# Attention weights folded ahead of the layers, and unscaled queries in a recurrence, in a two-block network on one core

## The chip, the cores and the metric

The kernel runs on one core of a Trainium2 chip. Its five engines (TensorE or PE, VectorE or DVE, ScalarE or ACT, GpSimd or POOL, SyncE or SP) each work through a list of their own, in order, and meet through semaphores. The metric is the device time of one execution in microseconds. The kernel before took 655.72 us (median of 3 runs, 652.77 to 656.79).

## The reference

The input x is 2 sequences of 1024 tokens of width 128, all in float32. Two blocks follow each other, each of the form x + attention(norm x) + experts(norm x).

```
# block 0
xn = layernorm(x)
q, k, v = xn Wq', xn Wk', xn Wv'
w[t,s] = exp(log(sigmoid(xn Wd' + bd) + 1e-8)[s] * max(s-t-1, 0)) * (s > t)
attn = ((q k' / sqrt(128)) * w) v Wo' * out_scale
ffn = xn, through 4 layers of: idx, p = top1(softmax(h @ router[l])) of 16 experts
                               h = p * silu(h @ W1[idx]) @ W2[idx]      (512 wide)
x = x + attn + ffn
# block 1
xn = layernorm(x);  ctrl = xn @ W_ctrl + b_ctrl      (9 parts)
q, k, v = silu(causal depthwise conv, 4 taps)        (16 heads of 8)
q = q / sqrt(sum(q*q) + 1e-12);  k likewise
per token: vec = u * rotate(vec @ W_block, angle) + (1-u) * silu(cand)
           S   = alpha * S + beta * k (v - S'k)';  read = S' q
attn = [rms(read) * w_m, rms(vec) * w_v] @ W_out + b_out, times sigmoid(gate)
ffn = p * (xn @ expert[top1]' + b)   of 8 experts
x = x + attn + ffn
```

Two identities matter to the change. Products of weights can be taken ahead: x Wq' (x Wk')' = (x Wq'Wk) x', and (x Wv') Wo' = x (Wo Wv)'. And rms(read) of a scaled query is read / sqrt(mean(read*read) + 1e-6 * (sum(q*q) + 1e-12)) of the unscaled one.

## The kernel before

**Front of block 0.** The 2048 tokens are 16 tiles of 128, in 4 groups of 4. SyncE loads x in four parts, then W2 in four parts (experts 0 to 1, 2 to 5, 6 to 10, 11 to 15), clears a scratch of 2 MB in HBM (`sorted_x<-slotbuf`), and loads W1 (4 MB). ScalarE issues nine small loads ahead of all else (L1682 to L1687: Wq, Wk, Wv, Wo, the first router, Wd, the later routers, bd, out_scale), 0.45 us each to issue and 0.68 for bd, which is spread over partitions. VectorE takes statistics (L975, L978) and scales rows (L988), group after group; GpSimd meanwhile makes constants (L703 the last long one).
TensorE's list starts when all nine loads have landed: transposes of the four attention weights (L2339), of tokens (L2126), the first layer's logits (L2135), ranks, and then a turn for each of 16 experts: transposes of W2 (L2222, copied by ScalarE at L1761) and W2 times the later routers (L2233, copied in turns by VectorE and ScalarE), so that each layer's output brings the next layer's logits with it. From expert 6 on a turn holds one of twelve attention products (L2247 queries and keys, L2250 values; VectorE copies them, L1119). VectorE also chooses and places each token by expert, and GpSimd scatters the rows into expert order (L737).

**Layers.** Each of 4 layers walks 31 tiles of 128 rows of sorted tokens: load, transpose (L2308), 8 products with W1 (L2317), SiLU, 8 with W2 (L2332), scatter (L748, L753). Between tiles stand pieces of the attention: scores (L2260), decay weights, retrieve (L2270), and the output product with Wo (L2283), 15 times, which VectorE adds to x (`attention_added`, L1244).

**Front of block 1.** GpSimd adds the expert rows to x, group by group; VectorE takes the mean (L1371, L1372), ScalarE the squares (L1879) and roots (L1698), VectorE scales (L1381), TensorE transposes and projects into the conv inputs (L2436, biased and copied by ScalarE at L1862). VectorE runs six convolutions (q, k and v for each of 2 sequences, each of three instructions of L1400 and L1403), with the angle range reduction after the second (L1422 to L1426, five instructions), then one rotation plane (`turn_plane`, L1414), the decay inputs (L1432) and the other plane. The recurrence is held with 32 chunks of 64 tokens on partitions: TensorE brings keys, queries and values into that form in four pieces each (`chunks`, L2451: 32 products of 128 partitions with a half of the identity); ScalarE squares (L1873) and copies them (L1874), GpSimd sums the squares (L820 to L822), ScalarE takes roots (L1935), VectorE reciprocals (L1442). GpSimd scales all queries by theirs (L847) before its first step.

**Recurrence.** 32 steps. In each VectorE computes prediction, difference and new state (L1510 to L1551), ScalarE the decayed state (L1948, eight pieces), GpSimd state times query (L864), TensorE sums it (L2561). Planes of the vector scan, routing (L1472 to L1493), experts (L2509, L2525) and gate stand between the steps at numbers written out by hand. GpSimd runs the vector scan (L784 to L790) from step 8 on. Behind the steps come a scan over chunks (L2670), corrections, mean squares, and the output projection.

## Time and profile before

| | us | share of span |
|---|---|---|
| median of 3 runs | 655.72 | |
| the profiled execution | 655.12 | |
| its span | 653.0 | |
| TensorE products | 566.2 | 87% |
| TensorE weight loads | 479.6 | 73% |
| VectorE | 475.1 | 73% |
| ScalarE | 427.5 | 65% |
| GpSimd | 383.4 | 59% |

The trace is of one execution; 2.1 us of its time lie outside the span. DMA moved 39.85 MB. Busy shares are means over stages with different limits; the slices show them: columns of 16.3 us each, tenths of the slice.

```profile
## 2 busy tenths in 40 slices
PE   0889999999999899989999589876965977798896
...
DVE  6655458865688457874312699799999999997946
ACT  1563567746675467645686688978877887786443
POOL 5354045710475025734555323786999999998984
PEclk9989999999999999979999698968979887989999
```

TensorE is full from the second slice to the twenty-second, VectorE from the twenty-fifth, GpSimd from the twenty-ninth. The chain that ended last gives TensorE 51%, GpSimd 21%, VectorE 18%.

### The profile page before, as it was taken

The page shows a single profiled execution, that of the slowest core. Times are in us where ns is not written, and L with a number is a line of the kernel's source. Part 1 is how long each engine was busy: PE and PEld are TensorE (multiplying, and loading weights), DVE is VectorE, ACT ScalarE, POOL GpSimd, SP SyncE. Part 2 cuts the span into 40 slices and gives each one's busy share as a digit, 9 for nine tenths or more (in the row PEclk, how much of TensorE's full clock was granted, in tenths as well). Part 3 has the DMA queues.
Part 4 walks back from the last instruction along what each step waited for, and adds up shares of the span by engine and source line. Part 5 has one row for each costly group of instructions (what it writes and reads, how often), then busy time and mean ns, then how long its engine had stood idle before and what let it go on. Part 6 is the DMA issues. An engine that isn't in the chain of part 4 may idle for free.

```text
span 653.0 us, 14371 instructions
## 1 busy us (share of the span) xinstructions
PE 566.2 (87%) x4639; PEld 479.6 (73%) x4639; DVE 475.1 (73%) x1380; ACT 427.5 (65%) x1032; POOL 383.4 (59%) x434
## 2 busy tenths in 40 slices
PE   0889999999999899989999589876965977798896
PEld 0767999769995899959997357744744755586785
DVE  6655458865688457874312699799999999997946
ACT  1563567746675467645686688978877887786443
POOL 5354045710475025734555323786999999998984
PEclk9989999999999999979999698968979887989999
DMA  8944553136321653125322000000000000000002
GB/s 291 346 149 47 161 120 66 55 58 166 74 65 46 92 147 65 54 55 74 71 53 77 23 1 2 1 2 1 1 0 2 1 1 1 1 2 1 3 2 66
DMA packets 104122, 39.85 MB, mean 61 GB/s; under 512 B 85906, under 2 KB 96178, under 8 KB 103922
## 3 DMA queue, kind: packets, MB, share of 16 engines
q1 hardware_dynamic: 98018, 29.34, 19.9%
q0 software_dynamic: 4480, 9.30, 4.2%
q8 instruction: 40, 0.66, 0.4%
q10 hardware_dynamic: 1552, 0.30, 0.2%
q14 instruction: 32, 0.26, 0.1%
HBM read 20.32 MB, written 18.59 MB: 60 GB/s over the span
## 4 chain that ended last, share of the span: by engine, by line
PE 51%; POOL 21%; DVE 18%; ACT 4%; issue 3%; DMA 2%; ACTq 1%; POOLq 0%; DVEq 0%; SPq 0%
PE PS L2332 17%; PE PS L2317 16%; POOL W1s L864 9%; DVE W2s L1403 4%; POOL wT L784 4%; PE PS L2270 2%; PE PS L2233 2%; POOL two_planes L786 2%; POOL slotbuf L788 2%; DMA oscale<-in_L_attn_out_scale_dram 2%; PE PS L2260 1%; ACT W1s L1948 1%; POOL hbuf L790 1%; POOL two_planes L789 1%; PE PS L2670 1%
## 5 line engine op out<-in xcount | busy, mean ns | idle before, releaser
L748 POOL DMA_INDIRECT sorted_x<-xrow,pos x93 | 90.9, 977 | 134.6 <-DVE pos L1216 107.8
L2332 PE MATMUL PS<-W2s,hbuf 128*128 x992 | 139.3, 284 | 0.0
L2317 PE MATMUL PS<-hbuf,swt 128*128 128x128 f32 x992 | 131.7, 276 | 1.0 <-DVE hbuf L1281 0.9
L2332 PEld LDWEIGHTS PS<-W2s,hbuf 128*128 128x128 f32 x992 | 126.7, 191 | 0.5
L2317 PEld LDWEIGHTS PS<-hbuf,swt 128*128 128x128 f32 x992 | 120.9, 192 | 1.6 <-issue 0.9
L1733 ACT ACTIVATE hbuf<-PS 128x512 f32<-128x512 f32 x124 | 73.2, 590 | 45.6 <-PE PS L2317 44.4
L1741 ACT ACTIVATE xrow<-PS,tags 128x144 f32<-128x144 f32 (+1 forms) x124 | 46.9, 378 | 41.8 <-PE PS L2332 39.6
L1948 ACT ACTIVATE W1s<-W1s,ab 128x128 f32<-128x128 f32 x168 | 51.3, 393 | 15.4 <-DVE W1s L1551 15.3
L2509 PE MATMUL PS<-ewT,xT 128*128 128x512 f32 x64 | 38.6, 734 | 21.0 <-ACT W2s L1999 21.0
L864 POOL TENSOR_TENSOR W1s<-W1s,kT 128x1024 f32<-128x1024 f32 x22 | 52.4, 2388 | 7.0 <-DVE W1s L1551 5.8
L753 POOL DMA_INDIRECT results<-xrow,pos x31 | 31.2, 1007 | 37.1 <-ACT xrow L1741 25.1
L1275 DVE COPY swt<-W1s 128x512 f32 x64 | 27.2, 427 | 35.2 <-PE PS L2317 33.2
L1284 DVE STREAM_TRANSPOSE hbuf<-hbuf 128x128 f32<-128x128 f32 x116 | 33.4, 301 | 23.0 <-DMA hbuf<-sorted_x 22.2
L2525 PEld LDWEIGHTS PS<-W2s,ident 128*128 128x128 f32 x256 | 34.9, 212 | 12.7 <-issue 12.4
L2561 PE MATMUL PS<-ident,W1s 128*128 128x128 f32 x256 | 34.8, 280 | 6.2 <-POOL W1s L864 6.2
L1815 ACT ACTIVATE swt<-W1s 128x512 f32 x60 | 37.9, 631 | 3.0 <-issue 1.0
L1999 ACT ACTIVATE W2s<-PS,selbuf 128x128 f32<-128x128 f32 x128 | 35.3, 370 | 5.0 <-issue 4.6
L2509 PEld LDWEIGHTS PS<-ewT,xT 128*128 128x128 f32 x64 | 12.9, 223 | 32.6 <-ACT W2s L1999 22.7
L2525 PE MATMUL PS<-W2s,ident 128*128 128x128 f32 x256 | 34.7, 294 | 2.0 <-DVE xres L1465 2.0
L2561 PEld LDWEIGHTS PS<-ident,W1s 128*128 128x128 f32 x256 | 29.2, 143 | 8.2 <-POOL W1s L864 7.5
L1948 ACT ACTIVATE W1s<-xrow,ab 128x128 f32<-128x128 f32 x88 | 26.9, 394 | 8.8 <-DVE xrow L1551 8.8
L1235 DVE SCALAR_TENSOR_TENSOR wdec<-PS,wdec 128x512 f32<-128x512 f32 (+3 forms) x24 | 13.4, 557 | 22.0 <-PE PS L2260 21.5
(419 smaller groups left out, 1324.4 us busy)
## 6 DMA issues: line engine op xcount, KB each, us to landing
hbuf<-sorted_x SPq DMA_DIRECT2D x224, 32.0 KB
sorted_x<-slotbuf SPq DMA_DIRECT2D x9, 520.0 KB, 2.9
W1s<-in_L_ffn_W_dram SPq DMA_DIRECT2D x1, 4096.0 KB, 20.6
sorted_x<-slotbuf SPq DMA_DIRECT2D x1, 2015.0 KB, 11.2
sorted_x<-xrow,pos POOLq DMA_INDIRECT x109, 2.4
sorted_x<-slotbuf SPq DMA_DIRECT2D x3, 455.0 KB, 2.8
xres<-in_L_attn_x_dram SPq DMA_DIRECT2D x4, 256.0 KB, 4.1
xrow<-results SPq DMA_DIRECT2D x4, 256.0 KB, 4.1
```

The costliest lines, as they stand in the source:

```text
L748: pool.indirect_dma_start(xs_dram[l + 1][:, :], bass.IndirectOffsetOnAxis(ap=pos[:, t:t + 1], axis=0), xrow[:, t % NR, 0:XW], None).then_i ...
L864: pool.tensor_tensor(qX[t % QR], X[(t + 1) % NX], Qc[:, t, :, :].unsqueeze(1).to_broadcast([P, 2 * HD, HP, HD]), ALU.mult).then_inc(r_read ...
L1733: act.activation(hTs[:, (c - 1) % 2, :], PS[:, 2 + (c - 1) % 2, :], ACT.Silu).then_inc(h_act, 1)
L1741: act.activation(xrow[:, t % NR, 0:w], PS[:, 4 + c % 2, 0:w], ACT.Copy, scale=tags[:, t, 1:2]).then_inc(y_ev, 1)
L1815: act.activation(w1st[:, c % WB, :], W1s[:, bass.ds(w, FF)], ACT.Copy).then_inc(w1_act, 1)
L1948: o = act.activation(aX[:, :, h, :], X[t % NX][:, :, h, :], ACT.Copy, scale=ab[:, t, h:h + 1])
L1999: o = act.activation(scaled[:, t % 2, e, :], PS[:, 4 + e // 4, e % 4 * D:(e % 4 + 1) * D], ACT.Copy, scale=sel[:, t, e:e + 1])
L2317: m = pe.matmul(PS[:, 2 + n, f * P:(f + 1) * P], w1st[:, (c - 1) % WB, f * P:(f + 1) * P], xring[:, (c - 1) % R, :], start=True, stop=True)
L2332: m = pe.matmul(PS[:, 4 + n, 0:w], hTs[:, n, f * P:(f + 1) * P], W2s[:, f * YW:f * YW + (E - 1) * NF + w][:, bass.ds(w2, w)], start=(f == ...
L2509: m = pe.matmul(PS[:, 4 + n, :], xT[:, t * P:(t + 1) * P], ewT[:, n * 512:(n + 1) * 512], start=True, stop=True)
L2525: pe.matmul(o, ident[:, :], scaled[:, t % 2, e, :], start=(e == 0), stop=False)
L2561: m = pe.matmul(o, qXw[t % QR][:, i, :], ident[:, :], is_transpose=True, start=(i == 0), stop=(i == HD - 1))
```

## The change

In the front, four small loads stay ahead (first router, Wd, bd, out_scale); the four attention weights and the later routers are issued by ScalarE after its table load, between its first roots, with a semaphore of their own. TensorE starts with tokens; then it waits for these five and makes Wq'Wk and a transpose of Wo (`folded_weights`), later Wo Wv (`folded_values`). The twelve attention products become eight: four give queries times the folded product, four give values times the folded one; ScalarE copies the first four, VectorE the rest. Scores take the tokens `xT` for the keys. The output product with Wo becomes a transpose. A long constant instruction of GpSimd waits for two scaled groups.

In block 1, norm groups 0 and 1 take their statistics on VectorE, with no squares on ScalarE, and group 0 ahead of an attention sum. Two of five range instructions go to GpSimd. The four key chunks stand together ahead of the third conv input, and a chunk is made of one 64x64 transpose and one 64x64 product a step. The decay inputs move ahead of the sixth convolution, the rotation planes into steps 2 and 3, the planes of the vector scan from steps 3 to 6 to 4 to 7. Queries stay unscaled: their lengths, reciprocal and scaling go; GpSimd squares them at step 1, TensorE sums them for step 4, and the sums, times 1e-6, are added into the mean squares.

```diff
+    QUERY_EPS_AT = 4
+    TURN_PLANE_AT = {2: 1, 3: 3}
...
+            pool.wait_ge(layer_x, 2)
...
-            pool.wait_ge(sincos, 2)
-            pool.tensor_tensor(cosp, cosp, cosp, ALU.mult).then_inc(cos_ready, 1)
-            squared_lengths(0)
+            pool.wait_ge(ang_red, 1)
+            step(pool.tensor_scalar(cosp, kp, -TWO_PI_LO, None, ALU.mult))
+            step(pool.tensor_tensor(angp, angp, cosp, ALU.add))
+            pool.tensor_scalar(angp, angp, PI_DOWN, -PI_DOWN, ALU.min, ALU.max).then_inc(ang_red, 1)
+            squared_lengths()
...
-            squared_lengths(1)
-            plane_summed(0)
-            pool.wait_ge(unit_ready, 2)
-            q_all = Qc.rearrange("p t h i -> p (t h) i")
-            step(pool.tensor_tensor(q_all, q_all, nstd[:, 1, :].unsqueeze(2).to_broadcast([P, C * HP, HD]), ALU.mult))
...
+                if t % (C // NG) == 0:
+                    pool.wait_ge(pa_ev, JOB_EV[f"q{t // (C // NG)}"])
...
+            dve.wait_ge(w_tr, 1)
+            dve.tensor_copy(wT[:, 0::3, :], PS[:, 5, :].rearrange("p (n d) -> p n d", n=4)[:, 0::3, :]).then_inc(w_ready, 1)
             first_place(0)
...
+            row_means(0)
             attention_added(4)
-            row_means(0)
             row_means(1)
+            row_scaled(0)
             attention_added(5)
             row_means(2)
-            row_scaled(0)
+            row_scaled(1)
             row_means(3)
-            row_scaled(1)
             row_scaled(2)
             row_scaled(3)
...
+            conv(0)
+            conv(1)
+            dve.wait_ge(pa_ev, 2)
+            step(dve.tensor_scalar(kp, angp, 1.0 / TWO_PI, ROUND, ALU.mult, ALU.add))
+            step(dve.tensor_scalar(kp, kp, ROUND, None, ALU.subtract))
+            dve.scalar_tensor_tensor(out=angp, in0=kp, scalar=-TWO_PI_HI, in1=angp, op0=ALU.mult, op1=ALU.add).then_inc(ang_red, 1)
+            conv(2)
+            conv(3)
+            conv(4)
+            decay_inputs()
+            conv(5)
+            key_lengths()
...
-            for n, w in enumerate(("Wq", "Wk", "Wv", "Wo")):
-                act.dma_start(wraw[:, n, :], ins[f"L0_attn_{w}"][:, :]).then_inc(ld_small, 16)
             act.dma_start(rw0[:, 0:E], routers[0, :, :]).then_inc(ld_small, 16)
...
+                if g < BY_STATS:
+                    act.wait_ge(centred, NG + g + 1)
+                    act.activation(stat[:, 2, tt], ex[:, tt, 7], ACT.Sqrt, bias=eps_ln[:, 0:1]).then_inc(ln_std, 1)
...
             preload(ACT.Sqrt)
+            own_weights(0)
+            own_weights(1)
             first_root(0)
+            own_weights(2)
+            own_weights(3)
             first_root(1)
+            act.dma_start(rw[:, 0:L - 1, :], routers[1:L, :, :].rearrange("l d e -> d l e")).then_inc(ld_own, 16)
             tokens_T(0, 0)
...
+            silu(1)
+            for g in range(NG):
+                chunked(0, Kc, g)
             conv_input(2, 0)
             conv_input(2, 1)
             silu(2)
-            chunked(0, Kc, 2)
             conv_input(2, 2)
             conv_input(2, 3)
             silu(3)
-            chunked(0, Kc, 3)
-            act.wait_ge(cos_ready, 1)
-            for n in (1, 3):
-                w = slice(n, n + 1)
-                act.activation(cos_part[n], cosp, ACT.Identity, bias=wblk[:, w], scale=n2wblk[:, w]).then_inc(cos_ready, 1)
-            silu(4)
-            silu(5)
+            act.wait_ge(ang_red, 2)
+            act.activation(cosp, angp, ACT.Sin, scale=0.5).then_inc(sincos, 1)
+            act.activation(sinp, angp, ACT.Sin).then_inc(sincos, 1)
+            preload(ACT.Sqrt)
+            lengths()
+            preload(ACT.Silu, 1)
...
+                if t == QUERY_EPS_AT:
+                    act.wait_ge(pd_mm, 6)
+                    act.activation(query_eps, PS[:, 1, 0:NT * H], ACT.Identity, scale=1e-6, bias=eps_q[:, 0:1]).then_inc(len_ready, 1)
...
-                    m = pe.matmul(PS[:, 7, t * P:(t + 1) * P], retT[:, (u % 2 * HB + t) * P:(u % 2 * HB + t + 1) * P],
-                                  wT[:, 3, :], start=True, stop=True)
+                    m = pe.transpose(PS[:, 7, t * P:(t + 1) * P], retT[:, (u % 2 * HB + t) * P:(u % 2 * HB + t + 1) * P], ident[:, :])
...
+            def folded_weights():
+                pe.wait_ge(ld_own, 16 * 5)
+                pe.matmul(PS[:, 5, 0:D], wraw[:, 0, :], wraw[:, 1, :], start=True, stop=True)
+                pe.transpose(PS[:, 5, 3 * D:4 * D], wraw[:, 3, :], ident[:, :]).then_inc(w_tr, 1)
+            def folded_values():
+                pe.wait_ge(w_ready, 1)
+                pe.wait_ge(xt_ready, 2)
+                pe.matmul(PS[:, ATTN_BANKS[0], 0:D], wraw[:, 2, :], wT[:, 3, :], start=True, stop=True).then_inc(w_tr, 1)
             pe.wait_ge(consts, 1)
-            pe.wait_ge(ld_small, 16 * 9)
-            for n in range(4):
-                m = pe.transpose(PS[:, 5, n * P:(n + 1) * P], wraw[:, n, :], ident[:, :])
-            m.then_inc(w_tr, 1)
             tokens_T(0, 0)
+            pe.wait_ge(ld_small, 16 * 4)
+            logits(0)
+            tokens_T(0, 1)
             second_T(0)
-            tokens_T(0, 1)
-            logits(0)
-            second_T(1)
+            folded_weights()
             pe.wait_ge(consts, 3)
-            second_routers(0)
             first_ranks(0)
             logits(1)
-            second_T(2)
+            second_T(1)
+            second_routers(0)
+            tokens_T(0, 2)
+            folded_values()
             second_routers(1)
-            tokens_T(0, 2)
             first_ranks(1)
-            second_T(3)
-            second_routers(2)
+            attention_in(0)
             tokens_T(0, 3)
-            second_T(4)
-            second_routers(3)
             logits(2)
-            second_T(5)
-            second_routers(4)
-            first_ranks(2)
-            for e in range(QKV_FROM, E):
+            for e in range(2, 6):
                 second_T(e)
-                second_routers(e - 1)
-                qkv(e - QKV_FROM)
-                if e == QKV_FROM + 2:
+                attention_in(e - 1)
+                second_routers(e)
+                if e == 2:
+                    first_ranks(2)
+            for e in range(6, E):
+                second_T(e)
+                if e > 6:
+                    second_routers(e - 1)
+                if e - 1 < 2 * NG:
+                    attention_in(e - 1)
+                if e == 8:
                     tile_row(0)
             second_routers(E - 1)
-            qkv(E - QKV_FROM)
-            qkv(E - QKV_FROM + 1)
-            pe.wait_ge(qkv_ready, 3 * NG)
+            pe.wait_ge(attn_ready, 2 * NG)
...
-                        for q in range(HS):
-                            m = pe.matmul(o[part_rows(q), t * DP:(t + 1) * DP], v, ident[:, part_rows(q)], start=True, stop=True)
+                        a, z = part_rows(0), part_rows(1)
+                        pe.transpose(o[a, t * DP:(t + 1) * DP], v[a], ident[a, a])
+                        m = pe.matmul(o[z, t * DP:(t + 1) * DP], v[z], ident[z, z], start=True, stop=True)
...
+            alpha_beta(range(8, 14))
+            chunks(0, range(NG))
             conv_input(2, 0)
             conv_input(2, 1)
-            chunks(0, (2,))
+            alpha_beta(range(14, 20))
             conv_input(2, 2)
             conv_input(2, 3)
-            chunks(0, (3,))
-            alpha_beta(range(10, C))
-            chunks(1, (0,))
+            alpha_beta(range(20, C))
+            chunks(1, range(NG))
...
+                if t == QUERY_EPS_AT - 1:
+                    pe.wait_ge(sq_ready, NG + 1)
+                    pe.wait_ge(sh1, 1)
+                    for n in range(NT):
+                        m = pe.matmul(PS[:, 1, n * H:(n + 1) * H], query_squares[:, n * P:(n + 1) * P], headsel[:, :], start=True, stop=True)
+                    m.then_inc(pd_mm, 1)
...
+                pe.matmul(PS[:, half, 0:G * H], ident[:, :], query_eps[:, half * G * H:(half + 1) * G * H], start=True, stop=False)
                 for t in range(G):
                     tt = half * G + t
-                    r = P // H
-                    m = pe.matmul(PS[:, half, t * H:(t + r) * H].rearrange("p (r h) -> p r h", r=r),
-                                  osq[:, tt * P:(tt + 1) * P], headmean[:, :].unsqueeze(1).to_broadcast([P, r, H]),
-                                  start=True, stop=True)
+                    m = pe.matmul(PS[:, half, t * H:(t + 1) * H], osq[:, tt * P:(tt + 1) * P], headmean[:, :], start=False, stop=(t == G - 1))
```

## Rows read from the trace of the kernel before

**Rows 1.** Chain of waits, first 68 us: start us, us, what.
```profile
4.87 9.99 DMA oscale<-in_L_attn_out_scale_dram
...
53.12 0.89 PE PS L2247 x2
54.01 0.44 PE PS L2222 x4
54.44 0.87 PE PS L2233 x8
```

**Rows 2.** Stage windows: stretch, length, busy (instructions) of five engines, clock, DMA, GB/s.
```profile
35.80:39.00 3.20, 3.20 (x24) 3.06 (x21) 2.54 (x12) 0.88 (x3) 0.00 (x0) 0.50 0.60 224
39.00:64.00 25.00, 23.98 (x166) 18.92 (x164) 12.92 (x35) 14.41 (x29) 14.32 (x43) 1.00 0.34 50
```

**Rows 3.** Timeline of the front: start us, us, engine, line, operation.
```profile
5.36 1.28 ACT L1724 ACT_TABLE_LOAD   x1 [5.36 <-issue]
...
7.37 2.44 DVE L988 TENSOR_SCALAR xrow<-xres,ex,stat 128x128 f32<-128x128 f32 x4
...
8.69 2.79 POOL L703 TENSOR_SCALAR dist<-hbuf 128x1024 f32<-128x1024 int32 x1
...
11.10 1.11 DVE L988 TENSOR_SCALAR xrow<-xres,ex,stat 128x128 f32<-128x128 f32 x4
...
64.11 0.44 PE L2308 MATMUL PS<-ident,hbuf 128*128 128x128 f32 x2 [0.78 <-DVE vtok L1119]
```

**Rows 4.** DMA: ScalarE's queue in 8:10 and 10:12 us; issues, us to landing.
```profile
q10 hardware_dynamic: 649, 0.02, 20.2%
...
q10 hardware_dynamic: 7, 0.00, 0.2%
...
sorted_x<-slotbuf SPq DMA_DIRECT2D x1, 2015.0 KB, 11.2
...
W1s<-in_L_ffn_W_dram SPq DMA_DIRECT2D x1, 4096.0 KB, 20.6
...
wraw<-in_L_attn_Wq_dram ACTq DMA_DIRECT2D x1, 64.0 KB, 2.3
```

**Rows 5.** Groups by line, ScalarE, 15 to 64.5 us: busy, mean ns, idle before.
```profile
L1761 ACT ACTIVATE retT<-PS 128x512 f32<-128x512 f32 x16 | 9.5, 593 | 15.1 <-PE PS L2222 15.0
```

**Rows 6.** Groups by line, TensorE, 138 to 352 us.
```profile
L2283 PE MATMUL PS<-wT,retT 128*128 128x128 f32 x30 | 4.0, 275 | 0.0
```

**Rows 7.** Chain of waits, 360 to 405 us.
```profile
362.28 3.19 ACT xT L1879 x16
...
375.47 1.29 DVE W2s L1403
...
404.87 1.42 DVE slotbuf L1414
```

**Rows 8.** Groups by line, VectorE, 374 to 415 us.
```profile
L1432 DVE TENSOR_TENSOR abraw<-PS,abbias 64x256 f32<-64x256 f32 x4 | 1.7, 422 | 0.1
...
L1425 DVE SCALAR_TENSOR_TENSOR retT<-dist,retT 128x1024 f32<-128x1024 f32 x1 | 1.2, 1226 | 0.0
L1426 DVE TENSOR_SCALAR retT<-retT 128x1024 f32<-128x1024 f32 x1 | 0.7, 697 | 0.0
```

**Rows 9.** Timeline of the second block.
```profile
385.58 4.27 PE L2451 MATMUL PS<-ident,W2s 128*64 128x64 f32 x64
...
415.30 0.69 DVE L1539 TENSOR_TENSOR W1s<-W1s,PS 128x512 f32<-128x512 f32 x1
...
424.48 1.75 DVE L1442 RECIPROCAL wraw<-wraw 128x256 f32<-128x256 f32 x1
...
448.08 2.38 POOL L864 TENSOR_TENSOR W1s<-W1s,kT 128x1024 f32<-128x1024 f32 x1 [5.76 <-DVE W1s L1551]
...
474.61 2.40 POOL L864 TENSOR_TENSOR W1s<-W1s,kT 128x1024 f32<-128x1024 f32 x1
...
607.75 0.29 PE L2670 MATMUL PS<-xT,W1s 64*64 64x64 f32 x4
```

More of the change, by code:

```diff
@@ L147, in build @@
     HALF = S // 512
[L148 removed]
+    assert ROUTE_AT < KB and B * NC * HS == P and B * (D // 2) == P and OFF[-1] == NCTRL
     assert at == C - 1 and len(EXPERTS_AT) == len(SUMS_AT) == NT and halves == 2 * NT
@@ L729, in second_block_masks @@
                 step(pool.memset(eps_col[:, :], 1e-6))
+                step(pool.memset(eps_q[:, :], 1e-18))
                 pool.memset(eps_kq[:, :], 1e-12).then_inc(consts1, 1)
@@ L866, in _ @@
                 if t < VEC_AT:
-                    if t == 2:
+                    if t == 0:
+                        pool.wait_ge(sincos, 2)
+                        pool.tensor_tensor(cosp, cosp, cosp, ALU.mult).then_inc(cos_ready, 1)
+                    elif t == 1:
+                        pool.wait_ge(post_ready, 2 * B)
+                        for b in range(B):
+                            half = slice(b * S, (b + 1) * S)
+                            o = pool.tensor_tensor(query_squares[:, half], post[1][:, half], post[1][:, half], ALU.mult)
+                        o.then_inc(sq_ready, 1)
+                    elif t == 3:
+                        plane_summed(0)
                         plane_summed(1)
@@ L1310, in _ @@
             route_tiles(0, NFG)
-            later_router(4)
-            for e in range(QKV_FROM, E):
-                qkv(e - QKV_FROM)
-                if e % 2 == 0:
-                    later_router(e)
-                if e == QKV_FROM + 2:
+            for e in range(4, E, 2):
+                for n in (e - 1, e):
+                    if BY_ACT <= n < 2 * NG:
+                        attention_in(n)
+                later_router(e)
+                if e == 8:
                     tile_table(0)
@@ L1415, in turn_plane @@
                                               op0=ALU.mult, op1=ALU.add))
-            dve.wait_ge(consts1, 3)
-            for k in range(3 * B):
-                conv(k)
-                if k == 1:
-                    dve.wait_ge(pa_ev, 2)
-                    step(dve.tensor_scalar(kp, angp, 1.0 / TWO_PI, ROUND, ALU.mult, ALU.add))
-                    step(dve.tensor_scalar(kp, kp, ROUND, None, ALU.subtract))
-                    step(dve.scalar_tensor_tensor(out=angp, in0=kp, scalar=-TWO_PI_HI, in1=angp, op0=ALU.mult, op1=ALU.add))
-                    step(dve.scalar_tensor_tensor(out=angp, in0=kp, scalar=-TWO_PI_LO, in1=angp, op0=ALU.mult, op1=ALU.add))
-                    dve.tensor_scalar(angp, angp, PI_DOWN, -PI_DOWN, ALU.min, ALU.max).then_inc(ang_red, 1)
@@ L1436, in _, with decay_inputs @@
-            o.then_inc(pd_ev, 1)
-            dve.wait_ge(conv_done, 3 * B)
-            def unit(n):
-                dve.wait_ge(len_ready, 2 * n + 2)
-                dve.reciprocal(nstd[:, n, :], nstd[:, n, :]).then_inc(unit_ready, 1)
-                dve.wait_ge(unit_ready, n + 1)
+            def decay_inputs():
+                dve.wait_ge(pd_mm, 4)
+                for q in range(HS):
+                    for k in range(2):
+                        half = part_rows(k)
+                        o = dve.tensor_tensor(abraw[part_rows(q), k * C // 2:(k + 1) * C // 2, :].rearrange("p t (n h) -> p t n h", n=2),
+                                              PS[half, 6, :].rearrange("p (t n q h) -> p q t n h", n=2, q=HS, h=HP)[:, q, :, :, :],
+                                              abbias[half, q, :].rearrange("p (n h) -> p n h", n=2).unsqueeze(1)
+                                              .to_broadcast([DP, C // 2, 2, HP]), ALU.add)
+                o.then_inc(pd_ev, 1)
@@ L1445, in next_keys, with key_lengths @@
+            def key_lengths():
+                dve.wait_ge(len_ready, 2)
+                dve.reciprocal(nstd, nstd).then_inc(unit_ready, 1)
+                dve.wait_ge(unit_ready, 1)
             def next_keys(t):
@@ L1954, in _, with rotation @@
             decayed(0)
-            for g in range(1, NG):
-                chunked(1, Qc, g)
+            def rotation(n):
+                if n == 0:
+                    act.wait_ge(sincos, 2)
+                    for i in range(2):
+                        act.activation(mpl[:, 0, i, :], sinp, ACT.Copy, scale=nwblk[:, 2 * i + 1:2 * i + 2]).then_inc(sincos, 1)
+                    return
+                for m in ((1, 3), (0, 2))[n - 1]:
+                    w = slice(m, m + 1)
+                    act.wait_ge(cos_ready, 1 if n == 1 else 3 + m // 2)
+                    act.activation(cos_part[m], cosp, ACT.Identity, bias=wblk[:, w], scale=n2wblk[:, w]).then_inc(cos_ready, 1)
             def plane_banks():
@@ L2014, in _ @@
                     reads_evac(t // G - 1)
+                if t in (0, 2, 3):
+                    rotation((t + 1) // 2)
+                if t in (1, 4):
+                    plane(zpl[:, t // 4, :], ACT.Silu, pbias[:, 2 + t // 4:3 + t // 4])
                 if t == 1:
-                    lengths(1)
-                if t in (2, 3):
-                    value(t - 1)
-                if t in (1, 2):
-                    plane(zpl[:, t - 1, :], ACT.Silu, pbias[:, 1 + t:2 + t])
+                    value(1)
+                elif t == 4:
+                    value(2)
+                    value(3)
                 if t == ROUTE_AT + 1:
```

249 lines of the change are left out of this document (124 added, 125 removed).

## The prediction, made before the result was known

> **What bounds the kernel now.** I read the slices of the page first, then the chain of waits, then for three stretches the stage windows, the timelines and the groups by line. Four stretches follow each other. (a) The front, to 64.11 us, where the first transpose of the first layer's tiles starts [rows 3]. TensorE does nothing until 14.99: its first instruction waits for all nine small loads of ScalarE's queue, and the last of them, oscale, takes 9.99 us to land [rows 1]. From 39 to 64 TensorE is busy 23.98 of 25 us at full clock [rows 2]; what ends there is its own list, turn after turn of 0.89 + 0.44 + 0.87 us [rows 1]. (b) Four layers to 352 us, TensorE busy from end to end. (c) The second block's front to 415.30, where the first state is written [rows 9]: the chain runs over VectorE's convolutions and then over ScalarE. (d) The recurrence, in which VectorE leads for nine steps and GpSimd from 474.61 [rows 9] to about 595, and the scan behind it. A gain in (a), (b) or (c) comes out at the end; in (d) it counts only if GpSimd starts earlier.
>
> **Front: the start.** Only four small loads stand ahead of the table load now: 0.45 + 0.45 + 0.68 + 0.45 us of issue (the 0.68 is the load spread over partitions) from 0.8, so to 2.9 us. Table load 1.28 [rows 3] and its 0.20: 4.4. Two weight loads are issued (0.95), then the root (0.3): 5.65. VectorE's statistics of two groups end at 6.4. Scaling of the first group took 2.44 us beside GpSimd's 2.79 us instruction at 8.69 [rows 3]; that one now waits for two groups, and the four scalings cost the 1.11 of the later groups. With the reciprocal: tokens at 7.8. TensorE: transposes 0.85 at the cold rate, copy 0.6, logits 0.85, second tokens 0.85, first W2 expert 0.5 to 0.9: about 12 us. What was done at 19.5 before is done at 12.
>
> **Front: the new wait.** Then TensorE waits for five loads (four weights, later routers), the last issued at 7.0 to 7.45. Behind that wait, in TensorE's order, stand ranks, logits and every later transpose; in VectorE's order the weight copy stands ahead of the first placing. The trace shows no load of this queue issued so late. From below: 7.45 + the 2.3 us of a weight load [rows 4] = 9.7, and TensorE would not notice. From above: oscale shows what happens to a tail that meets the 2 MB clearing transfer: 649 packets of this queue move in 8 to 10 us, 7 in 10 to 12 [rows 4]; the clearing lands at 4.06 + 11.2 = 15.3, oscale at 14.86. Behind it W2's stream keeps the engines full, so up to 18. I take **16**, nearest to oscale's row.
>
> The Trainium skill (DMA: Bandwidth & Descriptors, Queues, rings and completion order) says that each engine alternates between its queues packet by packet, whole packets of several descriptors. By it the 24 rows per engine of the last load want only two or so turns after the clearing: near 16 to 17, the same sum; it speaks against the slow rival below, as oscale's landing does.
>
> **Front: TensorE's list from there.** Fold and transpose 0.3, ranks 1.25 in all, logits 0.87 + 1.74, 15 W2 transposes at 0.44 = 6.6, 16 router products at 0.87 = 13.9, eight attention products at 0.89 = 7.1 (twelve before: keys are gone, 3.6 us), tokens 0.9, folded values 0.25, tile row 0.3: 33.2, so 49.2. The waits between: tokens and logits for ScalarE's copies 0.9; ScalarE's three table loads and two decays fall in turns that lost their attention product, 2.0 + 0.6 per turn against TensorE's 1.31, and cost it 1.3; hot masks and first copies 1.1; the last router copy 0.7. That gives 53.2. After an idle stretch the clock was 0.50 in 35.8 to 39 [rows 2]; a like phase after the new wait, about 1 us: **54.2**. Laid out in the same manner with these prices, the order before gives 64.2 (trace 64.11). Placing ends at 34.5, its last eight scatters at 1.27 us each at 44.7, tiles load 3 to 5 us later: covered, and so is W1, which lands at 39.8 [rows 4]. ScalarE has 0.6 [rows 5] plus half a router copy of 0.5 per turn: also under 1.31. So −9.9, with bounds −13.3 (landing before 13) and −7 (18, and a longer cold phase).
>
> **Layers.** 30 records of the output product [rows 6] become 15 transpose records; either kind runs at 0.11 us per record (0.87 for 8 products, 0.44 for 4 transposes [rows 1]). TensorE is the path there: −1.6; bounds 0 and −1.7. Scores read xT for kT: the same shapes, nothing.
>
> **Second block, norms.** For groups 0 and 1 the path was sum, negation, eight squares of 0.39 + 0.19 (3.19 us [rows 7]); now 1.25 us of statistics on VectorE, and group 0 no longer stands behind the attention sum. The first convolution still waits for groups 2 and 3, which keep the old way: start at 375.3 [rows 7] less 1.5.
>
> **Second block, convolutions.** Six of three instructions of 1.29 us [rows 7] stay. Two range instructions, 1.23 + 0.70 [rows 8], go to GpSimd, idle then; the decay inputs, 4 x 0.42 [rows 8], move ahead of the sixth; two plane turns (1.42 [rows 7] and 1.3) move into steps 2 and 3. The four key chunks now all stand ahead of the third conv input on TensorE and ScalarE: if a chunk costs what it did (64 records in 4.27 us for two [rows 9]: 2.15), the fifth convolution starts about 4.5 us late. The new form has 24 records on a 64x64 corner. The nearest row by shape is the scan's, 4 records on such a corner in 0.29 us with the next corner's beside them, some 0.03 us per record [rows 9]: 0.7. Bounds 0.7 and 2.15; I take 0.9, since transposes and products alternate between two corners as there. ScalarE's 1.05 per chunk is then longer, and VectorE loses 0.3 us.
>
> The Trainium skill (TensorE: Matmul & The Clock Gate, Part 3, The mechanism) has weight loads run beside products only on other row groups. Its Part 4 says that transposes do not count as busy for the clock. Here 0.44 per four transposes at granted clock 1.00 stands beside products; alone they would be a rival, below.
>
> From the sixth convolution to the first state: silu, value chunk, copy, eight decays of 0.3, 7 us. Against 415.30 that is −4.5 (with the norms). **Steps 1 to 4**: from 417.8 to 448.03 before, 30.2; now four of 5.07, routing 1.0, keys 0.45, choice 3.95, two turns 2.8: 28.5, since the query reciprocal (1.75 [rows 9]), the 3.8 us query scaling and its waits are gone. Steps 4 to 7 give about 2 back: the planes come one step later and ScalarE (2.45 + 2.1 + a 1.28 table load, values) is late for VectorE. GpSimd had no gap from 448.08 to 474.61 [rows 9]; it takes up two squares (4.8), the second sum and the cosine square earlier, while it waited anyway. Laid out so, step 9 starts at −4.3; the same layout gives 472.3 for 474.61 before. I take **−4**; bounds −6 (GpSimd alone) and +3 (chunks at 2.15). Behind it nothing moves; the mean squares have 10 short records for 8 long ones: 0.
>
> **Sum.** 655.1 (the profiled execution; 0.6 under the median of 655.7) −9.9 −1.6 −4 = **639.6**. A measurement tells about 1%, 6.6 us, from no change.
>
> **Rivals.**
> - *The late weights* (slower). If the five loads had to wait for the W2 and W1 stream to end, at 39.8, TensorE's list would start there: 54.2 + 23.8 = 78.0, that is +13.9 −5.6 = +8.3: 663. It breaks even at a landing of 31.5. For: the queue's 7 packets in 2 us. Against: oscale landed while W2 still streamed, and scatters landed in 2.3 to 5.3 us beside it. 6%.
> - *Nothing from the second block*: chunks near 2.15, or ScalarE late: +3 there: 646.6. For: ScalarE has hardly a gap in 404 to 420. 24%.
> - *The slow clock*: with attention products gone, turns 9 to 15 are half transposes; at 0.50, as in 35.8 to 39 [rows 2], their 9.2 us double: 648.8. Against: 39 to 64 is 1.00 with the same transposes. This is what the skill's Part 4 would make of it. 10%.
> - *The weights in time* (landing before 13): 3.4 more: 636. 15%.
> - The forecast: 45%.
>
> Range 633 to 650: below, the early weights with the full −6; above, either of the two middle rivals. Faster by over 1%: 0.89; within: 0.05 (two middle rivals together); slower: 0.06.
>
> **What would show it.** The first transposes near 8, the fold product near 16, the first layer near 54; 15 transpose records for the output; chunks at 16 transposes or products and 0.7 to 0.9 us; first state write near 399 on the new clock (415.3 −11.5 −4.5), GpSimd's ninth step 15.5 us earlier. A fold product after 20, a clock of 0.5 between 40 and 54, or VectorE waiting long for conv inputs would make it wrong.

## The result: slower by 4.4%, and where it went

The changed kernel takes 683.88 us (median of 4 runs, 682.69 to 684.68) against 654.76 (now 4 runs); the ratio is 1.044, with a 95% interval of 1.040 to 1.048, written [1.040, 1.048] below. The forecast was 639.6. Its profiled execution has a span of 681.4 us against 653.0: 28.4 us more. The page's slices of the changed kernel, columns of 17 us:

```profile
PE 612.8 (90%) x4554; PEld 504.6 (74%) x4554; DVE 467.8 (69%) x1381; ACT 425.2 (62%) x1019; POOL 385.2 (57%) x436
...
PE   2899999999999999999969999999867777798896
...
DVE  7644568755885578742067533488999999997936
...
PEclk9999999999999999899988575666998779989997
```

TensorE has 85 fewer records and 47 us more of work. In the slices that follow the layers it is full, its granted clock is at 5 to 8 tenths, and VectorE drops to 2 and 0. The waits of VectorE that end after 390 us and the timeline of TensorE name the place. Columns of the waits: who waited for whom, us in total, times, longest.

```profile
DVE PS L1545 <- ACT vtok L1944: 18.7, 1, 18.7
DVE W2s L1432 <- ACT W2s L1916: 17.4, 1, 17.4
```

Two waits, 36 us: the fifth convolution waits for its input, which stands behind the four key chunks, and the first step waits behind the four query chunks. The timeline of TensorE inside a key chunk, at its start and at its end:

```profile
376.59 0.27 PE L2517 MATMUL PS<-ident,W2s 64*64 64x64 f32 x1 [0.38 <-ACT W2s L1922]
376.79 0.43 PE L2518 MATMUL PS<-ident,W2s 64*64 64x64 f32 x2
377.14 0.27 PE L2517 MATMUL PS<-ident,W2s 64*64 64x64 f32 x1
...
396.67 0.32 PE L2517 MATMUL PS<-ident,W2s 64*64 64x64 f32 x1
396.92 0.48 PE L2518 MATMUL PS<-ident,W2s 64*64 64x64 f32 x2
397.32 3.78 PE L2502 MATMUL PS<-xT,wc 128*128 128x512 f32 x4
```

L2517 is the transpose, L2518 the product. A plain float32 product shows as two records, a transpose as one. One step takes 0.55 us at first and 0.66 later; a chunk 5.25, where it took 2.15 and 0.9 was forecast. The conv inputs behind the chunks run at half rate (3.78 us for four records; 1.98 in the trace of before). The stage windows, to be read as [rows 2]:

```profile
375.00:387.00 12.00, 11.62 (x60) 7.98 (x59) 9.38 (x9) 2.69 (x5) 6.18 (x3) 0.63 0.00 0
387.00:398.00 11.00, 11.00 (x49) 7.14 (x49) 0.00 (x0) 2.66 (x6) 0.00 (x0) 0.50 0.00 0
```

The granted clock is 1.00 from 372 to 376.5, 0.93 from 376.5 to 378.3 and 0.50 behind that: the first chunk had begun at full clock, and TensorE was full before the clock fell. Then 49 records filled 11 us.

The account by stages, each from the same events in both traces: first layer's transpose 58.24 for 64.11 [rows 3], −5.9; from there to the first convolution (364.80; 375.47 [rows 7]), −4.8; from there to the first state (435.74; 415.30 [rows 9]), +31.1; from there to GpSimd's last instruction of the steps (620.2; 594.9), +4.8; from there to the end, +3.1. Sum +28.3.

### The profile page after: what moved, and what is told of

Its sections match the earlier page's. It is cut to its first block, busy times and chain, and to the rows that moved or that the text cites. A ratio compares the mean times of both kernels' runs of the same rounds, so it can differ in the third digit from the quotient of the medians.

```text
span 681.4 us, 14191 instructions
## 1 busy us (share of the span) xinstructions
PE 612.8 (90%) x4554; PEld 504.6 (74%) x4554; DVE 467.8 (69%) x1381; ACT 425.2 (62%) x1019; POOL 385.2 (57%) x436
## 4 chain that ended last, share of the span: by engine, by line
PE 63%; DVE 21%; ACT 5%; issue 4%; DMA 3%; POOL 3%; SPq 0%; DVEq 0%; POOLq 0%; ACTq 0%
PE PS L2388 16%; PE PS L2373 16%; PE PS L2518 6%; PE PS L2517 3%; PE PS L2288 2%; PE PS L2575 2%; PE PS L2591 2%; DMA rw<-in_L_ffn_routers_dram 2%; PE PS L2502 2%; ACT W1s L1996 2%; DVE W1s L1583 2%; PE PS L2493 2%; DVE W1s L1552 2%; DVE PS L1554 1%; DVE PS L1556 1%
## 5 line engine op out<-in xcount | busy, mean ns | idle before, releaser
L775 POOL DMA_INDIRECT results<-xrow,pos x31 | 31.1, 1002 | 35.9 <-ACT xrow L1780 24.3
L2518 PE MATMUL PS<-ident,W2s 64*64 64x64 f32 x192 | 45.2, 333 | 0.0
L2591 PEld LDWEIGHTS PS<-W2s,ident 128*128 128x128 f32 x256 | 33.4, 204 | 12.7 <-issue 12.5
L2518 PEld LDWEIGHTS PS<-ident,W2s 64*64 64x64 f32 x192 | 28.1, 192 | 10.2
L2591 PE MATMUL PS<-W2s,ident 128*128 128x128 f32 x256 | 33.2, 286 | 1.9 <-DVE xres L1500 1.9
L2627 PEld LDWEIGHTS PS<-ident,W1s 128*128 128x128 f32 x256 | 30.9, 149 | 2.2 <-POOL W1s L884 1.5
```

What stands on the lines that cost most here:

```text
L2518: m = pe.matmul(o[z, t * DP:(t + 1) * DP], v[z], ident[z, z], start=True, stop=True)
L2591: pe.matmul(o, ident[:, :], scaled[:, t % 2, e, :], start=(e == 0), stop=False)
L2627: m = pe.matmul(o, qXw[t % QR][:, i, :], ident[:, :], is_transpose=True, start=(i == 0), stop=(i == HD - 1))
```

## The experiments

The runs fell into five groups: e1 to e4; e5 to e8; e9 to e12; e13 to e16; e17 and e18. Ratios are against runs of the kernel before in the same group. That matters: in the second and third group the kernel before took 701 and 694 us, with waits of up to 5 us in the layers whose cause the trace does not name, and 656 to 659 us in the others. It is not the chip alone: the third and the last group ran on the same one. In the second and third group only ratios and stretches without such a wait are read, and the kernel with two plain products, to which most of their edits were made, was not run beside them; so their ratios can't be set against its 0.986.

### What the chunk costs

Edit of the first (the second puts back the old form, the third first loops over the transposes, then over the products):

```diff
-    pe.transpose(o[a, t * DP:(t + 1) * DP], v[a], ident[a, a])
+    pe.matmul(o[a, t * DP:(t + 1) * DP], v[a], ident[a, a], start=True, stop=True)
     m = pe.matmul(o[z, t * DP:(t + 1) * DP], v[z], ident[z, z], start=True, stop=True)
```

> The changed kernel, with each step of a chunk made of two 64x64 plain products (four records) in place of one transpose and one product (three records). In the changed kernel a step takes 0.56 to 0.66 us and a chunk 5.25. Theory M: what costs is the change from transpose to product and back, twice in each step. Then the four records run as the scan's do, the two corners side by side, some 0.12 to 0.16 us per step and 1.0 to 1.3 per chunk, and the kernel takes 640 to 645 us. Theory C: records on a 64x64 corner cannot be laid beside each other here, whatever their kind. Then a step keeps 0.6 us or more, with four records perhaps 0.8, and the kernel takes 680 or more. Theory K (the clock): the chunks are slow because the granted clock is 0.5 there; then the chunk stays near 5 as long as the clock does.

> The changed kernel with the chunks in the form of before: two products over 128 partitions per step. All theories of the chunk agree: 2.15 us per chunk, key chunks over 8.6 us after they start in place of 20.7, and the kernel at 645 to 650 us. If the order of the second block (four key chunks ahead of the third conv input, planes one step later) is itself a cost, as the rival with chunks near 2.15 had it, the second block comes out about 3 us over before; then 648.

> The changed kernel with the same 24 records per chunk, but the eight transposes first and the eight products behind them, so that there is one change of kind per chunk and not sixteen. Theory M: about 0.11 us per record as in other rows, 2.2 to 2.8 us per chunk, the kernel near 650. Theory C: every record still waits for the one before it, 4.5 to 5.2 us per chunk, the kernel within 3 us of 684.

Measured: 646.66 us, ratio 0.986 [0.979, 0.993]; 648.67, 0.988 [0.981, 0.996]; 658.61, 1.004 [1.002, 1.007]. The timelines of TensorE, of the plain products (e1), of the grouped form (e3) and of the old form (e2):

```profile
376.80 0.27 PE L2517 MATMUL PS<-ident,W2s 64*64 64x64 f32 x1
376.81 0.27 PE L2518 MATMUL PS<-ident,W2s 64*64 64x64 f32 x1
376.91 0.27 PE L2517 MATMUL PS<-ident,W2s 64*64 64x64 f32 x1
376.92 0.27 PE L2518 MATMUL PS<-ident,W2s 64*64 64x64 f32 x1
377.02 0.27 PE L2517 MATMUL PS<-ident,W2s 64*64 64x64 f32 x1
```

```profile
379.59 1.06 PE L2516 MATMUL PS<-ident,W2s 64*64 64x64 f32 x8
380.58 2.04 PE L2518 MATMUL PS<-ident,W2s 64*64 64x64 f32 x16
382.55 1.06 PE L2516 MATMUL PS<-ident,W2s 64*64 64x64 f32 x8
```

```profile
376.81 8.17 PE L2517 MATMUL PS<-ident,W2s 128*64 128x64 f32 x128 [0.38 <-ACT W2s L1922]
```

In e1 the two corners start 0.01 us apart, and a corner's next record 0.11 after its last: a step of four records takes 0.22 us, a chunk 1.76. The old form takes 8.17 / 4 = 2.04. The Trainium skill (TensorE: Matmul & The Clock Gate, Why this matters for your kernels) has products on different row groups run at the same time; the trace agrees for two plain products (e1), and not for a transpose beside a product. Grouped, the changed kernel's 24 records take 2.96 us (379.59 to 382.55). So neither the corner nor either kind is dear, but the change between them. (The transposes all lie on one corner and the products on the other, so each of these changes is one of corner too; in e1 a change of corner alone costs nothing. A change of kind on one corner was not tried. On the full array it is free: in a turn of the front, four transposes between products take 0.43 us, 54.01 to 54.44 [rows 1].)

Theory K, the clock, is out as well. e1's granted clock is 0.51 from 377.4 to 379.6, and its records go on starting 0.11 apart. And where the changed kernel had the full clock inside a late chunk, the chunk was still slow:

```profile
449.80:453.10 3.30, 3.30 (x19) 2.54 (x18) 3.27 (x6) 2.92 (x9) 2.03 (x1) 1.00 0.00 0
```

19 records in 3.30 us make 4.2 for the 24 of a chunk, against 5.25 at half clock and e1's 1.76 for its 32 records. A dose in between:

```diff
-    for t in range(SB):
-        pe.transpose(...)
-        m = pe.matmul(...)
+    for t in range(0, SB, 2):
+        for k in (t, t + 1): pe.transpose(...)
+        for k in (t, t + 1): m = pe.matmul(...)
```

> The changed kernel with the records of two steps paired: two transposes, two products, and so on, 8 changes of kind per chunk where the changed kernel has 16 and the grouped form 2. Theory M, a price for each change of kind: chunks took 5.25 and 2.95 us with 16 and 2, 0.16 us for each change, so 3.9 to 4.0 us per chunk here, and the kernel between the two, near 669 us. If instead only the first change of a run is dear, or the overlap is lost altogether once kinds are mixed, the chunk stays above 4.8 and the kernel at 680.

The ratio is 1.035 [1.027, 1.042], which at the first group's 656 us would be about 678. The whole time was over the expected 669, the chunk was where it should be:

```profile
433.85 0.42 PE L2517 MATMUL PS<-ident,W2s 64*64 64x64 f32 x2
434.20 0.70 PE L2519 MATMUL PS<-ident,W2s 64*64 64x64 f32 x4
434.83 0.42 PE L2517 MATMUL PS<-ident,W2s 64*64 64x64 f32 x2
```

ScalarE's copies of its key chunks start 3.84, 3.95 and 3.94 us apart. With 16, 8 and 2 changes a chunk takes 5.25, 3.94 and 2.96: 0.16 us for each change, on a straight line (all three at a granted clock of 0.50). The stretch from the first convolution to the first state lies on it too: 70.9, 59.1 and 50.8 us. The expectation of 669 failed in the ratio of a slow group, not in the chunk.

### The front

The edits of e9 (the load moves) and of e10 (nine products in the wait; six in later runs), in one view:

```diff
-    act.dma_start(rw[:, 0:L - 1, :], ...).then_inc(ld_own, 16)      # behind first_root(1)
+    act.dma_start(rw[:, 0:L - 1, :], ...).then_inc(ld_own, 16)      # behind the first router's load
...
+    for n in range(9):
+        pe.matmul(PS[:, 7, 0:P], ident[:, :], ident[:, :], start=True, stop=True)
     folded_weights()
```

> The kernel before with the front of the change alone: four small loads first, own weights late, folded products, eight attention products, scores on the tokens, the output as a transpose. The trace of the changed kernel has the first layer at 58.2 us and the end of the layers' products at 341.0, against 64.1 and 351.45 before. If that gain of 10.4 us is handed on to the end, 643 to 646 us. If the second block or the last scatters behind the layers eat it, 650 or more.

> The kernel with two plain products per step, and the four attention weights and the later routers issued ahead of ScalarE's table load again, right behind the four small loads; TensorE's order stays the new one. In the changed kernel the last of them lands at 18.11 and the first layer starts at 58.24. Theory L (the late landing moved the front by its own length): they land near 15, TensorE waits 3 us less, and its first turns leave the half rate sooner; first layer 3 to 5 us earlier, 642 to 644 us. Rival: ScalarE's table loads and copies between 41 and 49 us bound the front whatever comes before; then the first layer moves by under 1.5 us and the time stays at 645 to 647.

> The kernel with two plain products per step, and of the five late loads only the one of the later routers (384 short rows) issued early, behind the first router; the four weights stay behind the table load. In the kernel with plain products the wait for the routers ended at 19.55 us and Wo, the last of the weights, landed near 15.4 in the changed kernel. Theory L (the last load's landing sets the front): the fold starts near 15.5, 3 us earlier or more, and the time falls by 2 to 4 us against the same kernel without it. Rival A (what the queue can move behind the 2 MB clearing, not the order of issue, sets the landing, as the run with all nine loads issued early hints, where it was 19.05): Wo takes the routers' place, the fold starts within 1 us of before, no gain.

> The kernel with two plain products per step, and nine plain products of the identity in a free bank while TensorE waits for its own weights (work that is thrown away). Theory W (TensorE comes out of that wait at the half rate, and its first turns at 18 to 27 us cost 3 us more for it: 1.65 us for eight router records that take 0.87 later): the turns after the wait run at 0.87, the first layer starts 2 to 3 us earlier, the time falls by 2 to 3 us. Rival: the rate stays low for as long after the wait whatever TensorE did in it, or the products outlast the wait: no change, or 1 us slower.

The front alone takes 645.65 us, 0.984 [0.978, 0.991]: its gain reaches the end. With all nine loads early 0.995 [0.992, 0.999], with the routers early 0.987 [0.983, 0.992], with products in the wait 0.994 [0.990, 0.999]; the last three are from the slow groups. The times alone therefore show no gain of the last three, and the traces have to. TensorE's timeline with early routers (e9), and with early products (e10, the thrown-away ones are L2411):

```profile
16.11 0.80 PE L2395 MATMUL PS<-wraw 128*128 128x128 f32 x2 [2.97 <-DMA wraw<-in_L_attn_Wo_dram]
...
17.22 1.87 PE L2190 MATMUL PS<-rw,xT 128*128 128x17 f32 x8
...
19.81 1.86 PE L2288 MATMUL PS<-rw,retT 128*128 128x96 f32 x8
```

```profile
12.97 3.71 PE L2411 MATMUL PS<-ident 128*128 128x128 f32 x18
16.97 0.49 PE L2395 MATMUL PS<-wraw 128*128 128x128 f32 x2 [0.28 <-DMA rw<-in_L_ffn_routers_dram]
...
17.61 1.04 PE L2190 MATMUL PS<-rw,xT 128*128 128x17 f32 x8
...
18.98 1.03 PE L2288 MATMUL PS<-rw,retT 128*128 128x96 f32 x8
```

From the fold to the first attention product it is 7.87 us in the one (23.98) and 4.95 in the other (21.92): 2.9 us of half rate are gone. The Trainium skill (TensorE: Matmul & The Clock Gate, Why this matters for your kernels) says that long idle gaps between bursts bring the rate down. No row here shows a fall: in the changed kernel the rate was low ahead of the wait already (four transposes from 11.38 take 1.09 us, as the four from 20.96 behind it do), and what the wait of 4.8 us did was to put off the rise. The profile's granted clock reads 1.00 from 18 to 28 us there, and that is no measurement: the trace holds its first clock entry at 26.5 us, the full level, just where the records become twice as fast (14.4 us in e18), and the view counts the time ahead of it as full.

The fold starts at 15.9 to 17.4 us in the six traces with early routers (mean 16.4), and at 17.0 to 19.6 in eleven with late ones (18.4). With all nine loads early it starts at 19.05 and 17.94 (e6, e8). So the order of issue alone does not bring the landing forward; taking the 384 short rows off the tail does, by about 2 us. Theory L in its plain form is wrong.

### Who sets the end of the recurrence

```diff
-    chunks(1, range(NG))
+    chunks(1, range(2))
     chunks(2, (0,))
+    chunks(1, range(2, NG))       # ScalarE's copies of these two behind decayed(0)
```

> The kernel with two plain products per step, with the first value chunk ahead of the third and fourth query chunks on TensorE and ScalarE, and those two behind the first decays. VectorE waited 2.5 us for that value chunk's copy before its first step. Theory V (VectorE is full from its first state to its last, so it sets the end of the recurrence, and GpSimd, which had slack of 1.7 us at the end, does not): what the first state gains comes out at the end, 1.5 to 2.5 us, 644 to 645 us. Theory G (GpSimd sets the end from step 9): the steps of GpSimd after the eighth do not move by more than their start does, and the first state's gain is lost where planes and values are late on ScalarE: within 0.7 us of 646.7.

> Both of the last two edits. The front and the second block stand one behind the other, so the two gains should add: 639 to 643 us by theories L and V, 645 to 647 by their rivals.

> The kernel with the first value chunk ahead of the third and fourth query chunks once more, since the chip of the last comparison was slower by 45 us for every kernel. Theory V (VectorE, full from its first state to its last, sets the end): 1.5 to 2.5 us less than the kernel with two plain products. Theory G (GpSimd from step 9): within 0.7 us of it.

> The last three edits together, with six thrown-away products in place of nine because the wait should be shorter. By theories L, W and V the gains of the first two overlap (both shorten the same stretch) and the third adds: 4 to 7 us under the kernel with two plain products, 640 to 643 us where the kernel before takes 656. By the rivals 645 to 647.

These fell into the slow groups: 0.995 [0.990, 1.000], 0.996 [0.992, 1.000], 0.998 [0.995, 1.001] and 0.994 [0.990, 0.998]. They tell no effect of 2 us. Once more, with the front's two remedies (early routers and six products in the wait), in a group that took 655.67 for the kernel before:

> The kernel before with the front of the change alone, the later routers issued early, and six thrown-away products in TensorE's wait. In the traces the fold then starts at 16.1 for 18 to 19.5 and the first attention product 5 us after the weights' landing and not 8. If the front hands these on: 4 to 5.5 us less than the front alone, which was 0.984 of the kernel before, so 0.976 to 0.978. If ScalarE's table loads at 41 to 49 us bound the front: 0.982 to 0.985.

> The changed kernel with two plain products, early routers, six thrown-away products and the first value chunk first. If VectorE sets the end of the recurrence, 1.5 to 2.5 us better than without values first, and together with the front some 6 us under the kernel with two plain products: 0.975 to 0.978 of the kernel before. If GpSimd does, 0.979 to 0.982.

> The kernel with two plain products and the first value chunk first, beside the same without it. Theory V (VectorE full from its first state to the last step, and GpSimd waiting for it at the end): 1.5 to 2.5 us less. Theory G: within 0.7 us.

> The reference of this comparison: the changed kernel with two plain products, 0.986 of the kernel before where it was measured first.

Measured: 641.98 us, 0.978 [0.972, 0.983]; 644.08, 0.984 [0.978, 0.990]; 648.07, 0.988 [0.983, 0.993]; 646.81, 0.990 [0.983, 0.997]. Values first brought nothing, and the wait it was to remove is still there (VectorE's waits of e15; 2.5 in e16):

```profile
DVE PS L1545 <- ACT vtok L1944: 2.6, 1, 2.6
```

ScalarE's timeline around that copy of the first value chunk, in e15 (values first) and in e16 (the order of the change):

```profile
398.45 1.05 ACT L1922 ACTIVATE W2s<-W2s 128x1024 f32<-128x1024 f32 x1
401.63 0.60 ACT L1944 ACTIVATE vtok<-PS 128x512 f32<-128x512 f32 x1 [2.13 <-PE PS L2519]
```

```profile
396.15 1.05 ACT L1922 ACTIVATE W2s<-W2s 128x1024 f32<-128x1024 f32 x1
397.10 1.08 ACT L1929 ACTIVATE kT<-PS 128x512 f32<-128x512 f32 x2
399.28 0.60 ACT L1944 ACTIVATE vtok<-PS 128x512 f32<-128x512 f32 x1 [1.10 <-PE PS L2518]
```

L1922 is the SiLU behind the sixth convolution, and the value chunk needs it. From its start to the copy it is 3.18 us in the one and 3.13 in the other: SiLU, 1.76 us of chunk, copy. The two query copies (L1929) stood in front of the value copy, but not in its way. VectorE begins 0.2 us after the copy ends in both (402.42; 400.08). GpSimd's scaling of the keys, for which VectorE also waits here, is not what it waits for last: of its two instructions the first, which VectorE needs, takes 0.6 us and is over at 398.83 in e16.

```profile
L864 POOL TENSOR_TENSOR wdec<-qT,abraw 128x1792 f32<-128x1792 f32 x1 | 3.3, 3309 | 0.0
...
L864 POOL TENSOR_TENSOR wdec<-qT,abraw 128x256 f32<-128x256 f32 x1 | 0.6, 627 | 0.1
```

So the edit did not bring the first state forward (39.5 us behind the first convolution with and without it), and theories V and G were not put to the test. From the first state to GpSimd's end it is 179.6 us in the old second block (before, e4 and e13: 179.6, 179.3, 179.7) and 180.4 to 182.1 with the new one (e1, e14, e15, e16), whose VectorE needs 176.5 to 179.0 up to its last state for what took 175.3. Both engines end within 4.5 us of each other; that neither alone would give anything is argued from this, not shown.

### What is worth keeping

The best front, the norm statistics of the change, and the second block otherwise as before; the second adds the plain 64x64 products in the old order.

```diff
+    BY_STATS = 2                  # with row_stats, norm_roots and the order of row_means of the change
...
-    m = pe.matmul(o[part_rows(q), ...], v, ident[:, part_rows(q)], start=True, stop=True)
+    m = pe.matmul(o[z, ...], v[z], ident[z, z], start=True, stop=True)
```

> The best front (front of the change, early routers, six thrown-away products) with one part of the second block: groups 0 and 1 of the norm by VectorE's statistics, in the order of the changed kernel. All else of the second block as before. The convolutions start 1.6 to 2.3 us earlier after the layers and nothing behind them is moved, so the end should be 1.5 to 2 us earlier: 640 us, 0.974 to 0.976 of the kernel before. If something behind the convolutions has its own time (a transfer, GpSimd), 0.978.

> The same, and each step of a chunk as two 64x64 plain products in the old order of jobs: a chunk costs TensorE 0.9 us for 2.15. VectorE waited 0.8 us for a conv input behind chunks before, and its last wait ahead of the first state was for GpSimd's keys: 0 to 0.8 us less than without it.

Measured: 641.29 us, 0.975 [0.970, 0.979], and 640.87 us, 0.973 [0.968, 0.978]. Both beat the kernel before and the changed one. The second's gain over the first is not told apart from none; its chunks start 1.8 us apart (370.46, 372.27), as in e1, and not the 0.9 expected.

## Why the prediction was wrong, step by step

**The chunk** is the step that failed. It said 0.7 to 2.15 us, "the nearest row by shape is the scan's", and took 0.9. The scan's records are all products. As two products the chunk takes 1.76; its corners do overlap, but a corner's records lie 0.11 us apart and the scan's some 0.06. (The chunk's source is strided, the scan's is not; whether that is the cause was not tried.) As a transpose and a product it takes 5.25. The bounds were drawn from rows of each kind by itself or of the two on the full array, and no row of before showed them alternating on corners. As a term of the sum it is 4.35 us for each of twelve chunks, the four key chunks on VectorE's path ahead of the fifth convolution and the query chunks ahead of the first state. The upper bound for the second block was +3; from the first convolution on +39 came.

**The slow clock** was priced as a rival in the wrong place. In the front's turns 9 to 15 the clock stayed at 1.00. It fell where the mixed chunks stood (from 378.0), and the conv inputs behind them paid double. It was a consequence and not the cause: a mixed chunk takes 4.2 us at the full level. It fell at the very end as well. Windows of the changed kernel (the like ones of before, 618 to 632 and 639 to 653, are both at 1.00):

```profile
646.00:660.00 14.00, 14.00 (x201) 12.69 (x199) 6.24 (x26) 5.59 (x13) 10.88 (x11) 1.00 0.01 2
...
667.00:681.00 14.00, 9.50 (x52) 8.90 (x52) 8.34 (x13) 2.39 (x6) 2.46 (x2) 0.76 0.25 75
```

That is the +3.1 behind the steps, where the forecast said "Behind it nothing moves". From GpSimd's last instruction to the end it is 57.9 to 59.3 us with the old second block (before, e4, e13, e17, e18); with the new one 61.2 to 61.9 in three traces (the changed kernel, e2, e15) and 58.4 to 60.0 in four (e1, e3, e14, e16) with the same instructions. In e1 the clock does not fall there, in e2 it does. So the fewer records of the mean squares do not settle it, and what makes the clock fall at the end is open.

**The front** came to 58.2 for 54.2: the last load landed at 18.11 for 16, and the turns after the wait ran at half rate until 26.5 us, 2.9 us for the 1 that was priced. ScalarE's table loads are in the chain from 41 to 49 us, but TensorE is busy 9.57 of 10 us there. The sum of TensorE's list held: with both remedies the first layer starts at 53.67 to 53.98 (e14, e17, e18; 56.97 in e13, where the rate stayed low). The rival of the late weights (landing at 39.8) did not come.

**Layers**: −1.6 forecast. With the old norms (e4, e13) the stretch to the first convolution is 3.4 and 4.0 us shorter. Groups by line, TensorE, 58.2 to 341 us:

```profile
L2327 PE MATMUL PS<-wdec,vtok 128*128 128x512 f32 (+3 forms) x34 | 17.2, 592 | 1.7 <-DVE wdec L1264 1.7
...
L2340 PE MATMUL PS<-ident,retT 128*128 128x128 f32 x15 | 2.3, 273 | 0.0
```

The 15 records are there, 1.7 us less than [rows 6]. The rest is shorter waits: in e4 TensorE waits 0.2 us for loads of sorted rows where it waited 1.7 before, and that was not in the forecast. **Norms**: with them that stretch is 305.2 to 306.8 us (the changed kernel, e1 to e3, e14 to e18) for 307.4 and 308.0: some 1.5 us, as forecast.

**Convolutions to first state** without the mixed chunks: 39.5 us for 39.8, where 3 us less were forecast (e16). The work left VectorE as said, 4.7 us of it. In its place stand waits of 1.3, 2.0 and 0.6 us for conv inputs and decay inputs, 2.5 us for the value chunk and 1.2 for the first decays behind it: 7.6 us, where before had 3.5. The first two are the four key chunks ahead of the third inputs, 4 x 1.76 = 7.0 us of TensorE where the forecast had 4 x 0.9 and charged 0.3. **Steps**: the forecast put the two turned planes inside steps at what they cost outside, and took VectorE for free behind step 9. It was within 4 us of GpSimd. So the rival with nothing from the second block fits e1 and e2 (+1.0 and +3.0 us over the front alone, which the intervals do not tell from nothing), and the forecast had 24% on it.

## What to carry to other kernels

Before replacing records by fewer ones, look whether the new sequence alternates kinds: a price per record from rows of one kind holds only there, and an unseen alternation needs its own bound. When a large order of work is moved at once, ask of each piece taken off the leading engine what that engine will wait for instead; here 4.7 us of work became 4 us of waits. A wait on TensorE early in a kernel cost its length and then 2.9 us more, because the rate had not risen yet. Before an edit is said to have tested a theory, look in its trace whether it moved what it was to move.

## What the runs showed of the hardware that was not expected

- A change between transpose and product on TensorE, on opposite 64x64 corners: 0.16 us each at half clock (16, 8 and 2 changes: 5.25, 3.94, 2.96 us). On the full array none is seen [rows 1].
- Plain products on opposite corners start 0.01 us apart (e1). Records of products in a row on one corner take 0.12 us each (16 in 1.97, e3).
- Six thrown-away products in the wait brought the full rate in three traces (e12, e17 and e18: 5.20, 4.95 and 4.96 us from the fold to the first attention product), part of it in a fourth (e14: 6.3), and none in a fifth (e13: 8.0). Nine did in the one trace that has them (e10: 4.95).
- The five weight and router loads of ScalarE's queue are in about 2 us later when 384 short rows are last than when a 64 KB weight is (18.4 and 16.4 us in the mean of eleven and six traces), and issuing them all early did not help (19.05, 17.94).
- The granted clock of a profile can lack its first entries: in the changed kernel it prints 1.00 up to 26.5 us, while records took twice their later time.
